# Projecting k for two batches at a time in three passes of high and low parts, in alternation with v

## What is computed

```python
q = layernorm(x) @ Wq            # 16 heads of 16 channels
k = ctx @ Wk
v = ctx @ Wv
p = softmax(q k^T / 4)           # over the 128 tokens of the context
x = x + tanh(g) * (p v) @ Wp
```

## Time and profile before

| | us |
|---|---|
| median of three runs | 2127.76 |
| lowest, highest | 2126.52, 2129.44 |
| the profiled execution: time, span | 2127.31, 2125.5 |
| TensorE busy in the span | 2039.2 (96%) |
| weight loads | 1794.9 (84%) |
| VectorE | 1756.2 (83%) |
| ScalarE | 1496.7 (70%) |
| GpSimd | 1217.2 (57%) |

### The profile page before, as it was taken

One profiled execution on the slowest core, in us unless ns is written; L12 is line 12 of the kernel. 1 busy time (PEld: TensorE's weight loads), 2 busy tenths in 40 slices (PEclk: granted clock), 3 DMA queues, 4 the chain that ended last, 5 costly groups with the idle time before them and its releaser, 6 DMA issues.

```text
span 2125.5 us, 57822 instructions
## 1 busy us (share of the span) xinstructions
PE 2039.2 (96%) x19788; PEld 1794.9 (84%) x19788; DVE 1756.2 (83%) x4916; ACT 1496.7 (70%) x3234; POOL 1217.2 (57%) x1800
## 2 busy tenths in 40 slices
PE   6999999999699999999799999999999999999997
PEld 5888888888599999999678888888788888888885
DVE  5889888898588888888677777777589999999996
ACT  4666666666478787878466666666668888888885
POOL 5788888878300000000277878877457777777776
PEclk9999999999799999999799999999999999999998
DMA  7555122221366666666422222222101100001000
GB/s 233 189 180 170 62 71 62 64 68 54 147 223 240 229 238 231 237 232 235 158 66 71 71 74 71 71 71 76 47 24 31 31 31 30 30 30 31 31 28 18
DMA packets 151665, 226.12 MB, mean 106 GB/s; under 512 B 20454, under 2 KB 135786, under 8 KB 141036
## 3 DMA queue, kind: packets, MB, share of 16 engines
q1 hardware_dynamic: 145260, 205.99, 28.8%
q0 software_dynamic: 6144, 16.79, 2.6%
HBM read 153.77 MB, written 68.94 MB: 105 GB/s over the span
## 4 chain that ended last, share of the span: by engine, by line
PE 87%; DVE 4%; issue 3%; DMA 2%; POOL 2%; ACT 1%; SPq 0%; POOLq 0%; ACTq 0%; DVEq 0%
PE ps L1254 11%; PE ps L1270 10%; PE ps L1126 10%; PE ps L1025 10%; PE ps L984 8%; PE ps L1111 6%; PE ps L1065 4%; PE ps L1202 3%; PE ps L1214 3%; PE ps L1158 3%; PE ps L1044 3%; PE ps L1059 2%; PE ps L1082 2%; PE ps L1095 2%; DMA slots_d<-rows,slot_s 2%
## 5 line engine op out<-in xcount | busy, mean ns | idle before, releaser
L1406 DVE TENSOR_REDUCE nmax<-ps 128x16 f32<-128x2048 f32 x128 | 292.4, 2284 | 29.7 <-PE ps L1082 29.3
L873 ACT ACTIVATE prob_t<-ps 128x2048 f32<-128x2048 f32 x128 | 240.9, 1882 | 77.5 <-PE ps L1065 77.5
L688 POOL COPY slot_in<-slot_all 128x1 int32<-128x1 int32 x64 | 11.4, 178 | 473.3 <-DMA eo_d<-eo 473.3
L1025 PE MATMUL ps<-w2f,a_t 128*128 128x256 f32 x1024 | 231.7, 379 | 0.3 <-ACT a_t L805 0.3
L1254 PE MATMUL ps<-xgt_hi,w_hl 128*128 128x256 f32 x1248 | 230.4, 283 | 1.0 <-DVE xgt_lo L1671 1.0
L1270 PE MATMUL ps<-w_hl,hid_hi 128*128 128x256 f32 x1248 | 226.9, 284 | 0.0
L1025 PEld LDWEIGHTS ps<-w2f,a_t 128*128 128x128 f32 x1024 | 189.6, 190 | 23.8 <-ACT a_t L805 0.6
L662 POOL TENSOR_TENSOR km_r<-qk,cst 128x512 fp32r<-128x512 f32 x128 | 133.5, 1043 | 126.1 <-ACT qk L863 126.1
L945 ACT ACTIVATE hid<-ps,b_in 128x256 f32<-128x256 f32 x312 | 146.1, 469 | 82.8 <-PE ps L1254 67.5
L1254 PEld LDWEIGHTS ps<-xgt_hi,w_hl 128*128 128x128 f32 x1248 | 195.7, 190 | 1.4 <-issue 1.4
L805 ACT ACTIVATE a_t<-ps,be_in,g_in 128x128 f32<-128x128 f32 x512 | 186.0, 470 | 12.2 <-PE ps L1044 11.3
(11 more groups left out here) (230 smaller groups left out, 6273.8 us busy)
## 6 DMA issues: line engine op xcount, KB each, us to landing
w_raw<-in_w_dram SPq DMA_DIRECT2D x78, 1024.0 KB, 6.8
c_t<-in_ctx_in_dram SPq DMA_DIRECT2D x128, 128.0 KB
x_d<-x SPq DMA_DIRECT2D x128, 128.0 KB, 2.4
slots_d<-zeros SPq DMA_DIRECT2D x12, 1024.0 KB, 6.1
eo_d<-zeros SPq DMA_DIRECT2D x12, 1024.0 KB, 5.6
xg<-slots_d SPq DMA_DIRECT2D x39, 256.0 KB, 2.8
eo_d<-eo SPq DMA_DIRECT2D x39, 256.0 KB, 2.2
x_in<-in_x_dram SPq DMA_DIRECT2D x64, 128.0 KB, 2.2
```

Of the source, the lines that this page charges most:

```text
L873: nc.scalar.activation(prob_t[:].rearrange("p a k -> p (a k)"), scores.rearrange("p a k -> p (a k)"), ACT.Exp, scale=SOFT).then_inc(y["exp ...
L1025: mm = pe.matmul(dst, a_t[:, b.parity, e, c, :], w2f[:, e, c, :], start=False, stop=True, skip_group_check=True)
L1406: nc.vector.tensor_reduce(nmax[:, b.parity, :, 0:4], scores.rearrange("p a (r k) -> p a r k", k=P), AX_X, ALU.max, negate=True).then_inc(y ...
```

## The change

k leaves the place between q and the transposed maxima. It is computed in three passes like v, for two batches at once: `wk_hi` or `wk_lo` is loaded as weights and the context of both batches, 256 columns, moves through. That is 12 matmuls for two batches into all 512 columns of `b5`. They stand at the end of TensorE's step, in odd steps s, for batches s+1 and s+2. v is computed for two batches as well (12 matmuls), at the end of even steps, for s-2 and s-1. q keeps its place and its four float32 matmuls.

The context is loaded in pairs, two steps earlier than before, as two pieces of 512 bytes in each partition, into two pair buffers; `c_hi` and `c_lo` are made in pairs of 512 elements in even steps and are held three pairs deep. ScalarE copies k (512 elements) at the head of even steps and v (512 elements) at the head of odd steps; q is copied alone (256 elements). At the head of a layer two instructions are added, the split of k's weights, and three waits for the split count to 4 where they counted to 2. The area of SBUF that the attention may use grows, and two buffers of the feed-forward move along with it.

The diff, cut to its core:

```diff
 # SyncE
-                    b = s + 1
-                    if b.within(B):
-                        if (b - 4).begun:
-                            sp.wait_ge(y["v_done"].of(b - 4), y["v_done"].at(b - 4))
-                        sp.dma_start(c_t[:, b.off % 4].rearrange("p c k -> p (c k)"), row(ctx_in, b)).then_inc(y["c_came"].of(b), 16)
+                    e = s + 3
+                    if e.off % 2 == 0 and e.within(B):
+                        if (e - 3).begun:
+                            sp.wait_ge(y["c_lo_done"].of(e - 3), y["c_lo_done"].at(e - 3))
+                        for t in range(2):
+                            b = e + t
+                            sp.dma_start(c_t[:, e.off // 2 % 2, :, t, :], row(ctx_in, b).rearrange("p (c k) -> p c k", c=C))\
+                                .then_inc(y["c_came"].of(b), 16)
...
                     if s.known and s.off == -1:
-                        sp.wait_ge(s_wv[n], 2)
+                        sp.wait_ge(s_wv[n], 4)
...
 # GpSimd
-                        pool.wait_ge(y["qk_out"].of(b), y["qk_out"].at(b, 1))
-                        masked(km_r[:, b.parity], qk[:, b.off % 4, 2:4, :]).then_inc(y["km_done"].sem, 1)
+                        pool.wait_ge(y["k_out"].of(b), y["k_out"].at(b))
+                        masked(km_r[:, b.parity], k_in[:, b.off // 2 % 2, :, b.off % 2, :]).then_inc(y["km_done"].sem, 1)
                         if (b - 2).begun:
                             pool.wait_ge(y["s2_done"].of(b - 2), y["s2_done"].at(b - 2))
-                        masked(qm[:, b.parity], qk[:, b.off % 4, 0:2, :]).then_inc(y["qm_done"].sem, 1)
...
+                        pool.wait_ge(y["q_out"].of(b), y["q_out"].at(b, 1))
+                        masked(qm[:, b.parity], q_in[:, b.off % 4]).then_inc(y["qm_done"].sem, 1)
+                    e = s + 2
+                    if e.off % 2 == 0 and e.within(B):
+                        r = e.off // 2 % 3
+                        pool.wait_ge(y["c_hi_done"].of(e + 1), y["c_hi_done"].at(e + 1))
+                        nc.gpsimd.tensor_tensor(c_lo[:, r], c_t[:, e.off // 2 % 2], c_hi[:, r], ALU.subtract)\
+                            .then_inc(y["c_lo_done"].sem, 2)
...
 # ScalarE
+                nc.scalar.activation(wk_hi[:], w_k[:], ACT.Copy).then_inc(s_wv[n], 1)
...
+                    e = s
+                    if e.off % 2 == 0 and e.within(B):
+                        act.wait_ge(y["k_done"].of(e + 1), y["k_done"].at(e + 1))
...
+                        nc.scalar.activation(k_in[:, e.off // 2 % 2].rearrange("p m t k -> p (m t k)"), b5, ACT.Copy).then_inc(y["k_out"].sem, 2)
+                    e = s - 3
+                    if e.off % 2 == 0 and e.within(B):
+                        act.wait_ge(y["v_done"].of(e + 1), y["v_done"].at(e + 1))
...
+                        nc.scalar.activation(v_aug[:, :, :, 0:DH], b5.rearrange("p (t h d) -> p t h d", t=2, h=H),
+                                             ACT.Copy).then_inc(y["v_out"].sem, 2)
...
-                        nc.scalar.activation(qk[:, b.off % 4].rearrange("p a k -> p (a k)"), b5, ACT.Copy).then_inc(y["qk_out"].sem, 1)
+                        nc.scalar.activation(q_in[:, b.off % 4].rearrange("p a k -> p (a k)"), b5[:, 0:2 * P], ACT.Copy).then_inc(y["q_out"].sem, 1)
...
 # TensorE
-                        projections(w_q, 0, x_t)
-                        pe.wait_ge(y["c_came"].of(b), y["c_came"].at(b))
-                        projections(w_k, 2, c_t[:, b.off % 4]).then_inc(y["qk_done"].sem, 1)
...
+                    e = s + 1
+                    if e.off % 2 == 0 and e.within(B):
+                        r = e.off // 2 % 3
+                        pe.wait_ge(y["c_lo_done"].of(e + 1), y["c_lo_done"].at(e + 1))
+                        for m in range(C):
+                            for c in range(C):
+                                for w, ct in ((wk_hi, c_hi), (wk_hi, c_lo), (wk_lo, c_hi)):
+                                    mm = pe.matmul(b5[:, m * 2 * P:(m + 1) * 2 * P], w[:, c, m * P:(m + 1) * P],
+                                                   ct[:, r, c].rearrange("p t k -> p (t k)"),
+                                                   start=(c == 0 and w is wk_hi and ct is c_hi), stop=(c == C - 1 and w is wk_lo))
+                            mm.then_inc(y["k_done"].sem, 1)
+                    e = s - 2
+                    if e.off % 2 == 0 and e.within(B):
...
 # VectorE
+                nc.vector.tensor_tensor(wk_lo[:], w_k[:], wk_hi[:], ALU.subtract).then_inc(s_wv[n], 1)
```

More of the change, by code:

```diff
@@ L135, in flamingo_gated @@
     CH = 4
-    ATTENTION_WORDS = 18432
-    QK_AT, PROB_AT = 7950, 12558
+    ATTENTION_WORDS = 20480
+    QK_AT, PROB_AT = 9998, 14606
     PARTS = 4
@@ L224, in flamingo_gated @@
         x_in = psb("x_in", [P, 8, D])
-        c_t = psb("c_t", [P, 4, C, P])
-        c_hi = psb("c_hi", [P, 2, C, P], F32R)
-        c_lo = psb("c_lo", [P, 2, C, P], F32R)
+        c_t = psb("c_t", [P, 2, C, 2, P])
+        c_lo = psb("c_lo", [P, 3, C, 2, P], F32R)
+        c_hi = psb("c_hi", [P, 3, C, 2, P], F32R)
         y_in = psb("y_in", [P, 4, D])
@@ L1121, in step @@
                         mm.then_inc(y["x2_turned"].sem, 1)
-                    def projections(w, part, src):
-                        for m in range(C):
-                            for c in range(C):
-                                mm = pe.matmul(b5[:, (part + m) * P:(part + m + 1) * P], w[:, c, m * P:(m + 1) * P],
-                                               src[:, c, :], start=(c == 0), stop=(c == C - 1))
-                        return mm
                     b = s
@@ L1132, in step @@
                         pe.wait_ge(y["x_t_done"].of(b), y["x_t_done"].at(b))
[L1133 to L1139 removed]
+                        if b.off % 2 == 0:
+                            pe.wait_ge(y["k_out"].of(b + 1), y["k_out"].at(b + 1))
+                        elif (b - 2).begun:
+                            pe.wait_ge(y["v_out"].of(b - 2), y["v_out"].at(b - 2))
+                        else:
+                            pe.wait_ge(y["q_out"].of(b - 1), y["q_out"].at(b - 1))
+                        for m in range(C):
+                            for c in range(C):
+                                mm = pe.matmul(b5[:, m * P:(m + 1) * P], w_q[:, c, m * P:(m + 1) * P], x_t[:, c, :],
+                                               start=(c == 0), stop=(c == C - 1))
+                        mm.then_inc(y["q_done"].sem, 1)
                     b = s - 1
@@ L1204, in step @@
                         mm.then_inc(y["pr_done"].sem, 1)
-                    b = s - 2
-                    if b.within(B):
-                        if (b + 2).within(B):
-                            pe.wait_ge(y["qk_out"].of(b + 2), y["qk_out"].at(b + 2))
-                        else:
-                            pe.wait_ge(y["v_out"].of(b - 1), y["v_out"].at(b - 1))
-                        pe.wait_ge(y["c_lo_done"].of(b), y["c_lo_done"].at(b))
-                        for c in range(C):
-                            for ct, w in ((c_hi, wv_hi), (c_hi, wv_lo), (c_lo, wv_hi)):
-                                mm = pe.matmul(b5[:, 0:D], ct[:, b.parity, c, :], w[:, c, :],
-                                               start=(c == 0 and ct is c_hi and w is wv_hi), stop=(c == C - 1 and ct is c_lo))
-                        mm.then_inc(y["v_done"].sem, 1)
+                    if s.off >= 0 and (s.off % 2 == 0 or (s + 1).within(B)):
+                        last = s if s.within(B) else At(0, B - 1)
+                        pe.wait_ge(y["q_out"].of(last), y["q_out"].at(last))
@@ new lines, in step @@
+                    e = s - 2
+                    if e.off % 2 == 0 and e.within(B):
+                        r = e.off // 2 % 3
+                        for t in range(2):
+                            for c in range(C):
+                                for ct, w in ((c_hi, wv_hi), (c_hi, wv_lo), (c_lo, wv_hi)):
+                                    mm = pe.matmul(b5[:, t * D:(t + 1) * D], ct[:, r, c, t, :], w[:, c, :],
+                                                   start=(c == 0 and ct is c_hi and w is wv_hi), stop=(c == C - 1 and ct is c_lo))
+                            mm.then_inc(y["v_done"].sem, 1)
```

59 lines of the change are left out of this document (24 added, 35 removed).

## The result

The changed kernel takes 2147.7 us (median of 4 runs, 2144.0 to 2148.1) against 2127.1 us (2124.7 to 2129.4) for the kernel before, run beside it: a ratio of 1.0093, with a 95% interval of 1.0076 to 1.0111. That is slower, by about 20 us, and above the range of the prediction (2110 to 2142). The profiled execution took 2148.1 us with a span of 2146.0.

The account below looks back on a forecast made before the run. TensorE's queue was the bound, with the reduction's loop taking over after the change. 2127.3 + 2.3 (layer 1) - 1.7 (layer 0) + 1.0 (ends) = 2128.9, forecast 2129 us; range 2110 to 2142, the forecast alone 2122 to 2137.

Parts of the forecast that it names:

- What bounds the kernel: TensorE's queue sets the step; behind it a loop, first scores through reduction to transposed maxima, has 0.73 us slack.
- The price of k's passes: On TensorE, k's new matmuls cost what v's do, 0.118 us apart; twelve take 1.51 us.
- the work saved: On TensorE, 0.19 us less work a step, 24 us over 128 steps.
- Layer 1, +2.3 us forecast: Layer 1's attention: TensorE waits for the maxima, the reduction's loop sets a 7.47 us step; +2.3 us over 58 steps.
- rival C: Layer 0: `km_r` follows `o_lo` at once and the pair's `c_lo` holds bookkeeping; first piece 9.90, +12 us, 2141; 22%.
- Layer 0, -1.7 us forecast: Layer 0's attention: cycle of four steps 32.95 us, -0.5 over 13 cycles; eight steps without bookkeeping win 0.15 each.
- first piece: Layer 0's cycle, reduction to reduction, bound by VectorE: 9.37 us before, taken as 9.0, between 8.65 and 9.37.
- Heads, +2.6 forecast: Start of each layer: k's burst and copy come ahead of the first q; +1.0 us each, up to +0.6 more in layer 0.
- Tails, -1.6 forecast: Step 63, the end of each layer's attention: no burst is left; -1.3 us in layer 1, -0.3 in layer 0.
- A: Rival: TensorE's work is the bound, the wait at the transposed maxima does not come or is made good; 2104 us; 8%.
- B: Rival: layer 0's bookkeeping slips out from under GpSimd's instructions, the first piece falls to 7.83, -16 us; 2114; 15%.
- D: Rival: k's passes cost more than v's or pairs come late; 0.05 us a step gives 2135, 0.1 gives 2142; 5%.

Follow-up runs that it names:

- the halves: Changed kernel with each burst of twelve k or v matmuls cut into six ahead of q and six behind the output projection: 2122.6 us, 0.9976 of the kernel before.
- the thin bursts: Changed kernel with the k burst of each layer's first two pairs cut from twelve matmuls to two (not a candidate): 2139.5 us, 1.0049 of the kernel before.
- all together: Changed kernel with bursts halved, `c_lo` in two, `km_r` held back in layer 1, VectorE's weight preparation behind `nmax_x`: 2112.4 us, 0.9920 of the kernel before.

## Why the prediction was wrong

The profiled execution took 19 us more than the 2128.9 of the sum. By the parts of that sum, 7.0 us are layer 1's steps, 6.7 the heads, 3.4 the tails and 1.5 layer 0.

- **What bounds the kernel**: right. That TensorE's saved work would bring nothing where it was put, since the loop of the reduction takes over, is what the halves show: with half of the same matmuls on the other side of the reduction the step falls by 0.24 us, from 7.47 to 7.23.
- **The price of k's passes** (1.51 us for twelve) and the work saved: right. TensorE's step with nothing in its way is 7.23 us; I had 7.24.
- **Layer 1, +2.3 us forecast, +9.3 measured**: the step of the loop, 7.47, was right to 0.01 us, and is the level of most steps of the runs with `km_r` held back. The failed step is the sentence that VectorE's other work and GpSimd's "have more room". 327 of 417 us is room on average. I had seen that `km_r` would follow `o_lo` at once and that L1191 would wait for `nmax_x`, put it into rival C, and priced it for layer 0 only, where the bookkeeping is. The forecast came to 431.9 + 2.3 = 434.2 us for the 58 steps; 441.3 were measured, and 434.8 with the gap in GpSimd's queue put back. So 6.5 of the 7.0 us missed are the held `xh`. The rest is of the size of the preparation pieces, to which the forecast gave no price: with their slack spent they cost 1.5 us (434.8 to 433.3, which is 58 x 7.47), where before they cost 0.9.
- **Layer 0, -1.7 us forecast, -0.2 measured**: the cycle was 32.97 for a forecast of 32.95, and its first piece, from reduction to reduction, 9.04 (305.92 to 314.96) for 9.0. The held operations are the ones described, longer by the longer `c_lo`; VectorE and GpSimd, to be read against the earlier trace rows:

```profile
305.92 2.29 DVE L1430 TENSOR_REDUCE nmax<-ps 128x16 f32<-128x2048 f32 x1
...
311.18 1.15 DVE L1465 TENSOR_SCALAR far<-kept 128x4 f32<-128x4 f32 x1
...
314.96 2.27 DVE L1430 TENSOR_REDUCE nmax<-ps 128x16 f32<-128x2048 f32 x1
```

```profile
311.00 1.30 POOL L730 TENSOR_TENSOR c_lo<-c_t,c_hi 128x512 fp32r<-128x512 f32 x1
```

  That the number fits is in part luck: 9.0 was chosen near the middle of 8.65 and 9.37. Of the terms, `c_lo` ended 6.38 us behind the reduction's start and not 6.2, and the next reduction came 2.66 later and not 2.45. Of the eight steps without bookkeeping four won 0.13 to 0.16 us each, as forecast; the next four, in which the bookkeeping begins, lost 1.1 together (8.67 and 9.63 us for 8.00 and 9.06). Why is not shown.
- **Heads, +2.6 forecast, about +9 measured**: mis-sized. The first burst was right: I counted 3.0 us at half clock, it took 2.7, and layer 0's first transposed maxima came 1.6 us later, as forecast (23.15 for 21.59). The second burst I did not count. It falls in the fill as well and made the next step 3.3 us longer (7.70 for 4.45); thinning both bursts gives back all of the 5.1 us. Part of it is the clock, which came to its full level later than before the change (last section): at 0.12 us from matmul to matmul the second burst would take 1.5 us and not 2.8. In layer 1 the lock comes on top:

```profile
1065.35 2.87 DVE L1438 TENSOR_SCALAR xh<-rows,mv,rs 128x256 f32<-128x256 f32 x1
...
1068.97 0.66 PE L1203 MATMUL ps<-cst,xh 128*128 128x128 f32 x2 [3.01 <-DVE nmax_x L1452]
```

  Holding `km_r` back gave 2.7 us of the 5.8 between the layers and the thin bursts 3.6, more than all of it together: the two overlap.
- **Tails, -1.6 forecast**: no gain. Layer 0's last four steps took 0.1 us more and its drain 1.2, layer 1's last stretch 0.5 more. Why the drain of layer 0 grew was not tried.
- **Rivals**: C had the sign and the mechanism, in the wrong layer, and its 2141 stands against 2148. In layer 0, where it was priced, its cycle of 33.6 us did not come (32.97). A and B did not happen. D (k's passes dear, pairs late) did not either: no wait for contexts or `c_lo` in the steady parts.

On the lock: in the held `xh` and `far` read here VectorE's end is within 0.2 us of the end of a GpSimd instruction on SBUF operands (1434.38 and 1434.23; 1390.80 and 1390.65; 312.33 and 312.30). Of the 77 `xh` of the changed kernel that took over 0.6 us, 76 end 0.15 or 0.16 us behind one. The Trainium skill, "SBUF — State Buffer", section "SBUF: two separate sides", gives the reason, a pair of ports that VectorE and GpSimd share as an exclusive lock for the length of an instruction. This case agrees and adds that the holder can pass it to itself: `xh` was overtaken by two more GpSimd instructions. That last point is read from the traces and was not tried by itself.

## What to carry to other kernels

Where one engine is full and a loop over another has little slack, ask of every move on which side of the loop the work lands: the changed kernel with its twelve matmuls in one place is 20 us slower than the kernel before, with the same twelve in two places it is 5 us faster. Two engines that share ports need the gaps between instructions counted, not busy time; a wait that is taken away can remove the gap in which the other engine got through, and putting it back was worth 12 us. Slack ahead of a held instruction hides the hold: with the bursts in halves, putting that gap back gained nothing in layer 1. A change that spends all the slack of a loop must be charged for every small irregular piece that the slack used to take, and one that makes bursts must be priced in the fill, where nothing hides them.

## What was not expected of the hardware

- A tensor_scalar of 256 elements on VectorE, 0.40 us alone, took up to 2.49 us behind three GpSimd instructions without a gap, and 2.87 us in the fill of layer 1, behind the gather (1064.88 to 1065.99), `km_r` and `qm`.
- The hold works both ways: while VectorE ran a piece on SBUF operands, GpSimd's one-element power took 1.66 us where 0.57 is usual, here in the run with `nmax_x` first; in the run with all together `qm` took 2.02 us instead of 1.04 beside a `w_lo`:

```profile
1383.94 1.15 DVE L1650 SCALAR_TENSOR_TENSOR b_hl<-b_hi,cst,b_lo 2x1024 fp32r<-2x1024 f32 x1
```

```profile
1383.87 1.66 POOL L677 TENSOR_TENSOR rs<-rs,cst 128x1 f32<-128x1 f32 x1
```

- The granted clock came to its full level later in the fills of the changed kernel. In layer 0 the kernel before has 2.4 GHz from 16.8 us on. The changed kernel has it from 16.9 to 20.3, then 1.2 GHz until 34.0. From 17 to 20 us TensorE was busy 1.5 of 3 us in both, so what made the clock fall in one of them is not shown. In the bursts of both heads k's matmuls were 0.21 us apart, and 0.12 later. Four kernels with the same bursts at the head came to full clock at 28.2, 32.4, 34.0 and 34.6 us, and their fills took 52.2, 52.4, 53.0 and 53.6. With the thin bursts it was 27.8, and the fill took 47.9 all the same. The columns are those of the earlier trace rows; before the change:

```profile
21.00:33.00 12.00, 9.44 (x114) 7.46 (x113) 9.06 (x13) 6.89 (x13) 8.66 (x13) 1.00 1.04 354
...
1065.00:1078.00 13.00, 10.75 (x162) 8.60 (x159) 9.53 (x14) 9.28 (x16) 9.32 (x15) 1.00 0.22 64
```

  After it:

```profile
21.00:33.00 12.00, 10.42 (x56) 8.56 (x59) 8.08 (x11) 3.94 (x9) 6.91 (x10) 0.50 1.07 379
...
1065.00:1078.00 13.00, 9.19 (x52) 7.13 (x52) 9.46 (x13) 3.83 (x7) 6.17 (x8) 0.50 0.37 119
```
